# Splitting W2 during the first two adjacency sweeps and keeping it in DRAM as 16-bit halves

## The reference, cut to what matters

```python
x = x + L0_gnn(layernorm(x), adj, W0, b0)        # A @ (xn @ W0 + b0) / column sums of A
x = x + L0_ffn(layernorm(x), Wg, bg, W1, b1, W2, b2)
#   gate = softmax(xn @ Wg + bg), the best 2 of 8 experts
#   h = gelu(xn @ W1[e] + b1[e]);  out += share_e * (h @ W2[e] + b2[e])
x = x + L1_gnn(layernorm(x), adj, WL, bL)        # relu of a normalised adjacency product
x = x + L1_ffn(layernorm(x))                     # a few flag and shift operations on columns
```

## Time and profile before

| | |
|---|---|
| median of 3 runs | 1075.37 us (1074.89 to 1077.36) |
| the profiled execution's own time | 1077.18 us |
| its span, first to last instruction | 1075.2 us |
| PE busy | 956.4 us, 89% |
| DVE, ACT, POOL busy | 559.4, 404.4, 360.0 us |
| bytes moved by DMA | 200.00 MB, mean 186 GB/s |

### The profile page before, as it was taken

One profiled execution on the slowest core, in us unless ns is written; L12 is line 12 of the kernel. 1 busy time (PEld: TensorE's weight loads), 2 busy tenths in 40 slices (PEclk: granted clock), 3 DMA queues, 4 the chain that ended last, 5 costly groups with the idle time before them and its releaser, 6 DMA issues. The chain is left out here.

```text
span 1075.2 us, 22179 instructions
## 1 busy us (share of the span) xinstructions
PE 956.4 (89%) x6724; PEld 627.4 (58%) x6725; DVE 559.4 (52%) x1643; ACT 404.4 (38%) x826; POOL 360.0 (33%) x416
## 2 busy tenths in 40 slices
PE   4988999999922799999999999999819999999993
PEld 1444544444411689898989898898704454444541
DVE  6734113127598566565656565665436334161754
ACT  4863758676787233232323232323112101010111
POOL 3510000014575345454545455454425320110110
PEclk9999999999965799999999999999959999999997
DMA  9785898899786423232332323232259978876771
GB/s 346 307 293 186 287 328 319 312 345 371 257 278 183 156 41 55 45 54 45 50 50 45 54 43 56 40 55 44 46 161 393 406 254 298 291 240 189 231 254 35
DMA packets 91265, 200.00 MB, mean 186 GB/s; under 512 B 13328, under 2 KB 47120, under 8 KB 91088
## 3 DMA queue, kind: packets, MB, share of 16 engines
q1 hardware_dynamic: 69248, 164.17, 43.5%
q0 software_dynamic: 17792, 31.02, 14.6%
q10 hardware_dynamic: 4176, 4.19, 1.2%
HBM read 176.41 MB, written 22.94 MB: 185 GB/s over the span
## 5 line engine op out<-in xcount | busy, mean ns | idle before, releaser
L921 PE MATMUL bank<-adj_f,feat 128*128 128x512 f16 x1024 | 240.8, 390 | 17.4 <-DMA adj_f<-in_adjT 15.7
L1202 ACT ACTIVATE act_f<-bank,b_sb 128x256 f32<-128x256 f32 x304 | 127.6, 471 | 288.4 <-PE bank L1148 288.4
L1148 PE MATMUL bank<-rT,experts 128*128 128x256 f16 x1824 | 207.8, 275 | 0.9 <-DVE rT L1215 0.9
L1169 PE MATMUL bank<-experts,act_h 128*128 x1824 | 205.3, 273 | 1.4 <-DVE y_f L1247 1.4
L1148 PEld LDWEIGHTS bank<-rT,experts 128*128 x1824 | 179.5, 98 | 22.9 <-issue 1.2
L1169 PEld LDWEIGHTS bank<-experts,act_h 128*128 128x128 f16 x1824 | 176.8, 98 | 21.6 <-issue 1.7
L1064 POOL DMA_INDIRECT x_rows<-y,token x76 | 121.9, 1604 | 193.1 <-DVE y L1254 165.2
L921 PEld LDWEIGHTS bank<-adj_f,feat 128*128 128x128 f16 x1024 | 97.5, 96 | 144.4 <-issue 18.1
L1588 PE MATMUL bank<-adj_g,feat 128*128 128x512 f16 x768 | 179.7, 387 | 0.3 <-POOL feat L1393 0.3
L805 ACT ACTIVATE spent<-adj_f 128x1024 f16<-128x1024 f32 x128 | 135.1, 1055 | 33.5 <-DMA adj_f<-in_adjT 28.3
L1588 PEld LDWEIGHTS bank<-adj_g,feat 128*128 128x128 f16 x768 | 73.8, 96 | 94.1 <-issue 0.8
(11 more groups left out here) (258 smaller groups left out, 910.0 us busy)
## 6 DMA issues: line engine op xcount, KB each, us to landing
adj_f<-in_adjT SPq DMA_DIRECT2D x128, 512.0 KB, 6.7
adj_g<-in_adjT SPq DMA_DIRECT2D x72, 512.0 KB, 6.0
adj_early<-in_adjT SPq DMA_DIRECT2D x24, 512.0 KB, 6.6
adj_g<-in_adjT SPq DMA_DIRECT2D x48, 256.0 KB, 3.1
unit_f<-in_W SPq DMA_DIRECT2D x16, 512.0 KB, 7.3
stage<-in_W SPq DMA_DIRECT2D x12, 512.0 KB, 7.0
x_ring<-in_x POOLq DMA_DIRECT2D x16, 256.0 KB, 7.6
x_rows<-agg SPq DMA_DIRECT2D x4, 1024.0 KB, 9.6
```

The source lines that it names most:

```text
L921: last = pe.matmul(mine(s)[ib * DC + c][:, :], feat0[:, j, h, c * P:(c + 1) * P], adj_0[j % RING][:, ib * HALF_SWEEP:(ib + 1) * HALF_SWEEP ...
L1148: last = pe.matmul(pb[2 + q][:, k * SLOT:(k + 1) * SLOT], w1_part(e * DC + (f // FQ * W2_UNIT0 + c), wh)[:, (f % FQ) * P:(f % FQ + 1) * P] ...
L1169: last = pe.matmul(pb[6 + r][:, 0:D], act_h[i][:, ah, f, r * P:(r + 1) * P], experts[:, ds(e * DC + (W2_UNIT0 + f // UH), 1), wh, (f % UH) ...
L1202: last = a.activation(act_f[q][:, k, :], pb[2 + q][:, k * SLOT:(k + 1) * SLOT], ACT.Gelu, bias=b1_sb[:, ds(e * FC + (2 * q + k), 1)], scal ...
```

## The change

W2 goes first. The 32 units get a new order q: the 16 units of W2 are q 0 to 15, W1's are q 16 to 31. ACT's multiplications stand behind tiles 18, 20, 21, 23, 24, 25, 27 to 31 of sweep 0 (q 0 to 10), every third tile of sweep 1 (q 11 to 21) and of sweep 2 (q 22 to 31). Units are loaded by POOL instead of SP, into a ring of four buffers in the memory where W1 will stand: the first four behind `split_row(28)` to `split_row(31)`, each later one when the unit four places earlier has been split. The halves of a W2 unit are made in one of two `parked` buffers and stored by POOL to a new DRAM tensor `w2_split`; ACT makes unit q only when the store of q - 2 has landed. DVE's splits of q 0 to 10 stand inside the loop over transposed rows (`SPLIT_BEHIND`). The last six W1 units use the two old buffers.

When sweep 3 is over, SP loads the halves straight into their place, two units (1 MB) in one transfer, the two that lie in `rows_late`'s memory after the rows are stored. `high_middle`, `split_middle`, `split_late`, both stage rings and the wait for `w2_parts` are gone. `x_ring` is loaded for row tiles 0 to 15 only, and `add_late_mean` adds `agg` itself.

```diff
-    for s, at in ((0, range(5, 30, 8)), (1, range(4, 30, 5)), (2, range(4, 30, 5))):
+    for s, at in ((0, (18, 20, 21, 23, 24, 25, 27, 28, 29, 30, 31)), (1, range(1, 32, 3)), (2, range(1, 30, 3))):
...
@@ sync
-                    if (s, j) in UNIT_AT:
-                        load_unit(UNIT_AT[s, j])
...
+            def load_w2(u, units):
+                k = u - W2_UNIT0
+                sp.dma_start(experts[:, u:u + units, :, :], w2_split[k:k + units, :, :, :].rearrange("u p h f -> p u h f")
+                             ).then_inc(sem("w2_loaded"), 16)
+            store_x1(0)
+            store_x1(1)
+            sp.wait_ge(sem("adj_used"), NS * NT + RING)
+            sp.wait_ge(sem("deg_ready"), NS * NT + RING)
             for k in range(4):
+                load_w2(W2_UNIT0 + 2 * k, 2)
+            store_x1(2)
+            store_rows(2)
+            for k in range(6, 8):
+                load_w2(W2_UNIT0 + 2 * k, 2)
+            store_x1(3)
+            store_rows(3)
+            sp.wait_ge(sem("late_stored"), 16 * 2)
+            for k in range(4, 6):
+                load_w2(W2_UNIT0 + 2 * k, 2)
...
@@ gpsimd
+            def load_unit(q):
+                if UNIT_RING <= q < RINGED:
+                    pool.wait_ge(sem("unit_lo"), q - UNIT_RING + 1)
+                if q >= RINGED + 2:
+                    pool.wait_ge(sem("unit_lo"), q - 2 + 1)
+                src = W2_u[q] if q < W2_UNITS else W1_unit[w1_unit_of(q)]
+                dst = unit_buffer(q)[:, :]
+                pool.dma_start(dst.rearrange("p (f d) -> p f d", d=D) if q < W2_UNITS else dst, src).then_inc(sem(unit_sem(q)), 16)
+            def park(q):
+                pool.wait_ge(sem("unit_lo"), q + 1)
+                pool.dma_start(w2_split[q, :, :, :], parked[q % 2][:, :, :]).then_inc(sem(f"parked{q % 2}"), 16)
             for n in range(NT):
                 split_row(n)
+                if n >= NT - UNIT_RING:
+                    load_unit(n - (NT - UNIT_RING))
...
             pool.wait_ge(sem("spare_zeroed"), 32)
+            for q in range(UNITS):
+                if q < W2_UNITS:
+                    park(q)
+                if q + UNIT_RING < UNITS:
+                    load_unit(q + UNIT_RING)
...
-                    load_x_again(G + n // 2)
...
@@ vector
-            split_unit(0)
-            split_unit(1)
+            SPLIT_BEHIND = {2: 0, 4: 1, 6: 2, 11: 3, 14: 4, 17: 5, 22: 6, 25: 7, 28: 8, 30: 9, 31: 10}
             for n in range(NT):
                 take_transposed(n)
...
-                if n == 18:
-                    split_unit(2)
+                if n in SPLIT_BEHIND:
+                    split_unit(SPLIT_BEHIND[n])
             split_w0g()
             take_x_gates()
-            split_unit(3)
...
@@ scalar
+            def high_unit(q):
+                a.wait_ge(sem(unit_sem(q)), unit_loads(q))
+                if 2 <= q < W2_UNITS:
+                    a.wait_ge(sem(f"parked{q % 2}"), q // 2 * 16)
+                if q >= RINGED:
+                    a.wait_ge(sem("unit_lo"), RINGED)
+                    for k in range(2):
+                        a.wait_ge(sem(f"parked{k}"), W2_UNITS // 2 * 16)
+                a.mul(unit_out(q, 0), unit_in(q), WS).then_inc(sem("unit_hi"), 1)
```

More of the change, by code:

```diff
@@ L152, in w1_part @@
         return w1_flat[:, ds(half * 2 + h, 1), :].rearrange("p a f -> p (a f)")
-    stage = [Region(X_AT + 16384 + k * 4096, end)(f"stage{k}", [P, 1024], F32) for k in range(MIDDLE_RING)]
-    late_stage = [Region(W_AT - 16384 + k * 4096, W_AT)(f"late_stage{k}", [P, 1024], F32) for k in range(UNITS - LATE_UNIT0)]
+    unit_ring = [Region(at, X_AT)(f"unit_ring{k}", [P, 1024], F32)
+                 for k, at in enumerate(W_AT + row * 1024 for row in (8, 12, 40, 44))]
+    parked = [Region(W_AT + row * 1024, X_AT)(f"parked{k}", [P, 2, 1024], F16) for k, row in enumerate((28, 60))]
     LATE_AT = W_AT - 16384
@@ L277, in program, with w1_unit_of, unit_buffer, unit_sem @@
     UNIT_AT = {}
-    for s, at in ((0, range(5, 30, 8)), (1, range(4, 30, 5)), (2, range(4, 30, 5))):
+    for s, at in ((0, (18, 20, 21, 23, 24, 25, 27, 28, 29, 30, 31)), (1, range(1, 32, 3)), (2, range(1, 30, 3))):
         for j in at:
             UNIT_AT[s, j] = len(UNIT_AT)
[L281 to L290, removed]
+    RINGED_W1 = (0, 1, 2, 3, 8, 9, 10, 11, 12, 13)
+    LAST_W1 = (4, 5, 6, 7, 14, 15)
+    RINGED = W2_UNITS + len(RINGED_W1)
+    assert len(UNIT_AT) == UNITS == RINGED + len(LAST_W1) and NS == 4 and RING == G
+    def w1_unit_of(q):
+        return (RINGED_W1 + LAST_W1)[q - W2_UNITS]
+    def unit_buffer(q):
+        return unit_ring[q % UNIT_RING] if q < RINGED else unit_f[(q - RINGED) % 2]
+    def unit_sem(q):
+        return f"unit_loaded{q % UNIT_RING}" if q < RINGED else f"last_unit_loaded{(q - RINGED) % 2}"
+    def unit_loads(q):
+        return (q // UNIT_RING if q < RINGED else (q - RINGED) // 2) * 16 + 16
+    def unit_out(q, h):
+        return parked[q % 2][:, h, :] if q < W2_UNITS else w1_v[:, w1_unit_of(q), h, :, :]
+    def unit_in(q):
+        return unit_buffer(q)[:, :] if q < W2_UNITS else unit_buffer(q)[:, :].rearrange("p (h f) -> p h f", h=2)
     def place(n):
@@ L435, in _ @@
                     store_pair(n - 1)
-                    load_x_again(G + n // 2)
[L438 to L445, removed]
-                low_row(n)
[L447 to L452, removed]
+            for n in range(2 * G, NT):
+                low_row(n)
             for k in range(2):
@@ L490, in rows, with split_unit @@
                                     ).then_inc(sem("xn_ready"), 1)
-            def split_unit(u):
-                v.wait_ge(sem("unit_hi"), u + 1)
-                v.scalar_tensor_tensor(out=unit_out(u, 1), in0=unit_in(u % 2), scalar=WS, in1=unit_out(u, 0),
+            def split_unit(q):
+                v.wait_ge(sem("unit_hi"), q + 1)
+                v.scalar_tensor_tensor(out=unit_out(q, 1), in0=unit_in(q), scalar=WS, in1=unit_out(q, 0),
                                        op0=ALU.mult, op1=ALU.subtract).then_inc(sem("unit_lo"), 1)
@@ L588, in _ @@
                 low_sums(s - 1)
-                u = UNIT_AT[s, 4]
-                split_unit(u)
+                first = UNIT_AT[s, 1]
+                split_unit(first)
                 for k in range(OT):
                     take_rows((s - 1) * OT + k)
-                    if k % 2:
-                        split_unit(u + 1 + k // 2)
-                split_unit(u + 5)
+                    if k % 3 == 1:
+                        split_unit(first + 1 + k // 3)
+                for q in range(first + 4, min(first + 11, UNITS)):
+                    split_unit(q)
             st = Steps(v, sem("v_norm1"))
@@ L872, in _ @@
             high_sums(3)
[L874 to L883, removed]
             for n in range(3 * G, NT):
@@ L1255, in take_y @@
                                     ).then_inc(sem("y_scaled"), 1)
-            v.sem_inc(sem("w2_parts"), LATE_UNIT0 - W2_UNIT0)
-            for k in range(UNITS - LATE_UNIT0):
-                split_late(k)
             next_rows(0, 0)
```

75 lines of the change are left out of this document (9 added, 66 removed).

## The result

The median run takes 1106.03 us (1103.89 to 1107.91, four runs) where the kernel before takes 1076.36 (1074.89 to 1078.59) beside it: a ratio of 1.0273, 95% interval 1.0242 to 1.0304. The change costs 30 us; 23 were forecast. A ratio is taken over the rounds, so it can differ from that of two medians in the fourth digit. The page counts 182.70 MB read and 31.33 written, 14.7 MB more than before (176.41 and 22.94).

A forecast was written before the change was run, and what follows sets the result against it. PE was taken to bound sweep 1 and the experts, DVE the routing, with waits in late sweep 0. Terms 10.0 + 6.0 + 6.8 + 1.2 + 2.0 + 0 - 3.0 gave +23.0, 1098.4 us; own range 1091 to 1108, wider 1083 to 1119.

The forecast's parts named there:

- b0 late: Sweep 0 behind tile 21: b0, queued behind four unit loads on POOL, lands late and PE waits 12.4 us; +10.0 us.
- First store late: Sweep 0, tile 22: unit 0's store waits for the zeroed spare rows, delaying ACT, DVE's split and PE's copies; +6.0 us.
- the first rival: Sweep 0: transfers issued from POOL land in 3.4 us, so the loss is +13, 1088 us; chance 0.19.
- Splits on PE's path: Sweep 0: seven visible splits between copies at 0.97 us each, +6.8, and unit 10's before the gate numbers, +1.2 us.
- Pace of the stores: Sweep 0, units 3 to 9: two buffers taking turns make the stores late, with a landing near 5.5 us; +2.0 us.
- Sweeps 1 to 3: The adjacency sweeps after sweep 0: the added loads and stores cost PE nothing; 0 us, sweep 1's bounds 0 and +18.
- the second rival: Sweeps 0 and 1: the added bytes bind, 6 us more in sweep 0, 18 in sweep 1; +47, 1122 us; chance 0.13.
- The middle: Sweep 3's end to PE's first transposes: earlier barrier and faster gather issue, less SP's traffic; -3.0 us, bounds -1.0 and -3.6.
- the fourth rival: Sweep 3's end to first transposes: gathers lose to SP's transfers what they win; +26, 1101 us; chance within the forecast's 0.60.
- The third rival: Sweep 0: idle time covers the waits and splits, leaving only the middle's 3 us gain; 1072.4 us, chance 0.08.

The follow-up runs named there:

- the control: The changed kernel unaltered, run again as the measure for spans: 1103.95 us, ratio 1.0252 to the kernel before.
- E1: Changed kernel with the b0 load and the spare rows' zeroing moved behind row 28, ahead of the first unit load: 1101.73 us, ratio 1.0206.
- E2: Changed kernel with four parked buffers instead of two: 1097.41 us, ratio 1.0166.
- E7: Changed kernel with early unit loads and bias, four parked buffers, unit 10's split behind the gate numbers, SP's four tiles behind the first gathers: 1072.45 us, ratio 0.9961.
- E3: Changed kernel with SP's four early adjacency tiles held back until PE's first transposes: 1100.33 us, ratio 1.0193.
- E6: Kernel before with only the bias and the zeroed rows issued behind row 28 instead of row 31: 1072.21 us, ratio 0.9954.
- E12: E6 with DVE's four late splits moved behind the first gathered token rows: 1070.6 us, ratio 0.9942.
- E8: E2 with each of DVE's splits 0 to 10 made twice: 1100.98 us, ratio 1.0238.
- E11: E7 run again unaltered: 1072.67 us, ratio 0.9961.

## Why the prediction was right, and where it was not

The direction, the place and roughly the size of the whole hold: 30 us slower for 23 forecast, sweep 1 at 126.16 where "near 125" stood, inside the forecast's own range (1106.0 in 1091 to 1108). Term by term it is less good, and the size is in part luck: errors in both directions cancel.

- **b0 late, +10.0:** 10.2 measured, and as written up to the issue: ACT stands 7.64 us for unit 0 and goes on at 59.36 (60.0), b0's load is issued at 66.00 (66.4). The landing is not as written: it takes 8.6 us, not 5.8, and PE goes on at 74.67, not 72.2. The wait of 12.55 meets the forecast's 12.4 only because PE came to the end of tile 21 2.3 us later than assumed; in the control it is 14.89. And the terms are not independent, which the sum assumed: E1 shows 1.4 to 4 us back when the wait goes.
- **First store late, +6.0:** 2.6 measured. The store landed 3.2 us behind the start of its issue (75.42; ACT goes on at 78.67), not 6.2. Of the 2.6 us, 0.7 are tile 22's matmuls at a lower clock (3.57 for 2.91). With b0 2.5 us later than forecast, tile 23 still begins at 83.44 where 84.4 was forecast: the two errors cancel. The Trainium skill ("DMA: Bandwidth & Descriptors", section "Anatomy of one DMA — SWDGE (gpsimd) path") gives 2.0 us and the bytes at 436 GB/s, an estimate of 3.2 us; that agrees with this one store, and not with the medians, 8.5 us for a unit load and 6.5 for a store. By these the first rival, short landings, is out.
- **Splits on PE's path, +8.0 with unit 10:** the mis-sized term. One row, 0.97 us in the earlier trace rows, was multiplied by seven. E2 has every split in its place and loses at most 3.1 us; E7, with unit 10's moved away, loses 1.2 (31.94 for 30.74). E2's trace shows one that ends beside a tile's eight matmuls. The one row was a copy that came late for PE once, and said nothing of the others.
- **Pace of the stores, +2.0:** the other mis-sized term, in the other direction and below the truth even at its upper bound of 7.4. Two buffers cost 10 us between tile 23 and sweep 1 (E2 against the control). The landing had been taken at 5.5 for a median of 6.5. The stores of units 2 to 10 leave POOL from 83.23 to 124.62, 5.2 us for each, the pace of the forecast's upper bound (5.15); but beside it PE's tiles need 3.4 (30.74 for nine), not the 4.1 that had a split in each. The two errors cancel, and only so is the +10.0 near 12.0. Of the 12.0, 1.6 are one tile at the lower clock (3.57 for 1.97).
- **Sweeps 1 to 3, 0:** +1.3, all in sweep 1's first five tiles, 10.50 us where 9.21 were, at a granted clock of 0.87 instead of 1.00. The clock covers it (0.87 of 10.50 is 9.1). With a DMA share of 0.99 PE stays busy 64.0 of 64, so the second rival, 18 us in this sweep, is out: at 371 GB/s no adjacency tile came late.
- **The middle, -3.0:** the step that failed. The barrier came earlier as forecast (first tokens 2.6 us behind PE's last matmul for 3.6), and the gathers are issued in 1.07 and 0.99 us for 1.82 and 1.89. Both are issued 62.6 us behind the end of sweep 3 for 65.0, a gain of 2.3 where 3.1 was forecast. The step put the loss to SP's traffic at 2 us at most; the landing takes 5.8 us for 1.9, and E3 measures 3.8. So the middle is +1.6 instead of -3.0, beyond the bound of -1.0 and beyond the fourth rival, which had it at nothing.
- **The third rival, covered:** false for the kernel as it is, for the reason given (the fixed orders). It is nearly true of E7: with loads early enough, four buffers and the gathers first, sweep 1 starts at 96.63, 2.5 us behind the same early bias alone (E6), and the middle pays that back.

The rule of the Trainium skill ("SBUF — State Buffer", section "SBUF: two separate sides"), that GpSimd's descriptors wait while VectorE holds the shared port, is borne out where it was tested: gathers issued from POOL take 1.8 to 1.9 us beside DVE's splits and 1.0 to 1.1 without (E6 and E12). What it would cost the 32 unit loads and 16 stores no experiment isolates; they are issued in 0.54 to 0.90 us here.

**Open.** The exact price of a hidden split (4.3 us for eleven by E8's trace, 7.8 by ratios of two sets). Why the clock behind sweep 3 was 1.00 in three profiles and 0.77 in the others. How much of E7's and E11's second wait ahead of sweep 1 (1.54 and 2.25 us for the last copy) comes from the longer landings: no run takes that apart.

## What to carry to other kernels

Moving work to an idle stretch is bought with the order of the engines that carry it: a load that waits, placed ahead of a small one that the critical engine wants, costs the whole landing, and the fix is the place, not the bytes (the 30 us of loss are PE's waits and the lower clock behind them; with 14.7 MB more no adjacency tile came late). Don't multiply one visible wait by the number of such instructions; look for what lies beside each, and put the doubt into how many buffers the slowest transfer takes turns in. Waits on one chain hide one another, so take them out together before you call the change bad, and then try the same repair in the kernel before: here it gave all of the gain. A wait read from one profile can be short by chance: 2.39 us in the first, 3.34 and 3.71 in the next two.

## What was not expected of the hardware

A wait of PE can cost more than its length. Behind the 12.55 us for b0, and again behind 2.92 us, eight matmuls that take 1.97 us take 3.57; the granted clock of those stretches is 0.50, the lower of its two levels (1.2 of 2.4 GHz), and 1.00 in the next tile:
```profile
77.50:80.90 3.40, 3.40 (x12) 1.15 (x10) 1.18 (x2) 2.14 (x4) 1.30 (x2) 0.50 0.84 304
83.50:85.30 1.80, 1.80 (x13) 0.76 (x10) 0.10 (x1) 1.80 (x4) 1.03 (x2) 1.00 1.06 405
99.90:103.20 3.30, 3.30 (x11) 1.05 (x8) 0.41 (x1) 1.82 (x2) 0.42 (x1) 0.50 0.99 323
```
In the kernel before 2.39 us of wait are followed by a tile of 2.91 us; in E6 without that wait it takes 1.97. The cost doesn't follow the length: behind the control's 14.89 us the tile takes 2.71, and behind the 1.66 us ahead of sweep 1 the kernel before has 9.21 us for 40 matmuls at a clock of 1.00.

Two transfers of 128 rows, wanted at once, take 5.8 us to land beside 2 MB from another queue, and 2.0 us alone (E3). The large transfer was in no hurry: in E3 it goes out 65.7 us behind the end of sweep 3 instead of 59.0, and from the first transposes on that kernel takes 719.3 us, as before.
